# A gated cross-attention block: rows centred but not scaled before the scores, the deviation moved into the exponential's scale, and batch 1's low parts made by VectorE

## The chip, the cores and the metric

One NeuronCore of a Trainium2 chip runs the whole kernel. The metric is the device time of one execution in microseconds (us). Three runs of the kernel before gave 129.15, 129.49 and 129.62 us, median 129.49.

## The reference

Two batches of 1024 rows of 256 numbers go through one gated cross-attention layer and one gated feed-forward layer with fixed-point rounding. Only the first half is touched by the change.

```
h   = (x - mean(x)) / sqrt(var(x) + 1e-5)             # per row of 256
q   = h @ Wq;  k = ctx @ Wk;  v = ctx @ Wv             # 8 heads of 64, ctx has 77 rows
a   = softmax(q @ k.T / 8)                             # per head
x   = x + tanh(g_xattn) * (concat(a @ v) @ Wo + bo)
y   = (x - mean(x)) / sqrt(var(x) + 1e-5)
h1  = relu(quant(quant(y) @ quant(w1).T + quant(b1)))  # 1024 wide
x   = x + tanh(g_ffn) * (quant(h1) @ quant(w2).T + quant(b2))
```

## The kernel before, in words

The 2048 rows are 16 tiles T of 128 rows, eight per batch. Two products of weights with the short context are made once per batch: `a_sb` (Wq times the keys, 256 x 616, so that scores are one product of the row with it) and `u_sb` (the values times Wo, 640 x 256, so that the attention's output is one product of the probabilities with it). Both are kept as a high part in float32r and a low part, the rest that float32r leaves out; the rows and the probabilities are split in the same way, and each product is three products: high x high, high x low, low x high (`PARTS`). A high part is a copy out of PSUM by ScalarE (`a_copy`, `u_copy`, `xT_copy`, `pT_copy`). A low part is a subtraction by VectorE out of PSUM (`a_low`, `u_low`, `rowsT_low`, `probsT_low`).

Batch 1 departs from this at three places. For `a_sb` c = 0 and c = 1 and for the middle piece of `u_sb`, ScalarE makes a second, unrounded copy of the PSUM bank in SBUF (`full`, lines 488, 493, 499), and GpSimd subtracts the high part from it (`a_low`, `u_low` at lines 293 to 301). GpSimd cannot read PSUM. The semaphores `copied` and `copied_low` carry that.

Everything is written by hand, with one instruction stream for each engine and semaphores between them. A loop over s = 0 .. 15 is unrolled on all engines. In step s, TensorE makes: the transposes of the rows of tile s+3 (`rowsT`, line 728), the transposes of the probabilities of tile s (`probsT`, line 755), extra work in early steps (line 699 for batch 1's `a_sb` in steps 0 and 1, line 835, line 712 for batch 1's `u_sb` in step 3), from step 4 a half of the feed-forward's hidden layer (line 803), the transpose of the second norm's result of tile s-2 (`quantisedT`, line 784), from step 6 the second layer of the feed-forward (line 818), the scores of tile s+2 (line 743), and the attention's output of tile s (`attend`, line 776).

VectorE's step s: `residual(s-1)` (584), `stats_second(s-1)` (589, 591), `denominators(s+1)` (554, 557), `probsT_low(s)` (579), `rowsT_low(s+3)` (570), in steps 3 and 4 `u_low` of batch 1, from step 6 `result(s-6)` (596), in steps 1 to 5 the first norm's statistics of two tiles (534, 537), and `center(s+2)`, the maxima and their subtraction (542, 547).

GpSimd's step s: `normalise_first(s+4)` (272), `normalise_second(s-1)` (283, 284, 286, 290), `softmax_scale(s+1)` (277), a low part of batch 1 in steps 0, 1 and 3 (295, 300), the widening of the hidden layer's int8 (322), `add_bias(s-1)` (343). `rstd_first` (263, 264, 266), the first norm's deviation, comes in steps 2, 4 and 6, for 2, 4 and 4 tiles.

ScalarE's step s: `exponentials(s+1)` (396), `pT_copy(s)` (408), `xT_copy(s+3)` (392), copies and roundings of weights in some steps, `hidden_round` (422) and `rowsT_second` (428).

Ahead of the loop TensorE runs six matmuls of constants that nobody reads (`WARM`, line 685), then the context's transposes (854), the keys (692), Wq's transposes (868), batch 0's `a_sb` (699), the values in two halves (692), the transposes of tiles 0 and 1 (881), `scores(0)`, `rowsT(2)`, batch 0's `u_sb` (712) and `scores(1)`.

## Time and profile before

| | us |
|---|---|
| median of three runs | 129.49 |
| the profiled execution | 129.84 |
| its span on the engines | 127.9 |
| TensorE busy | 121.3 (95%) |
| VectorE busy | 99.8 (78%) |
| GpSimd busy | 93.7 (73%) |
| ScalarE busy | 71.3 (56%) |

The profiled execution took 129.84 us, of which 127.9 are the span from the first to the last instruction. Busy shares are averages over a start (up to 22 us), a loop and a tail, each with its own limit. TensorE's matmuls are pipelined, so that its 95% hides short waits; they are read from the start of one group of matmuls to the start of the next.

### The profile page before, as it was taken

What the parts mean: (1) busy time and instruction counts of PE and PEld (TensorE: products, weight loads), DVE (VectorE), ACT (ScalarE), POOL (GpSimd) and SP (SyncE); (2) the same over time, 40 slices, a digit from 0 to 9 for tenths busy, and PEclk for the clock granted to TensorE, in tenths of its full rate; (3) what the DMA queues carried; (4) which work ended last, traced back from release to release, by engine and by line L of the source; (5) the groups of instructions that cost most, each with busy time, mean ns of one, the idle gap of its engine ahead of it and who ended that gap; (6) DMA issues with size and microseconds to landing.
All of it is one profiled execution on the core that took longest, in us unless ns stands there. A gap on an engine that the chain in (4) does not pass through costs nothing.

```text
span 127.9 us, 2834 instructions
## 1 busy us (share of the span) xinstructions
PE 121.3 (95%) x996; PEld 110.4 (86%) x996; DVE 99.8 (78%) x221; ACT 71.3 (56%) x151; POOL 93.7 (73%) x175
## 2 busy tenths in 40 slices
PE   7999999999995999999999999999999999999990
PEld 2698978989893799999999899999999999888780
DVE  6109888599999879999897969697887979547882
ACT  4124625599793828499392829282837546365520
POOL 3002873777979898989998998988768596987720
PEclk9999999999999999999999999999999999999999
DMA  3898898100000000000002000200020020001014
GB/s 113 244 297 300 292 399 350 68 3 5 3 3 0 0 0 8 0 0 0 5 0 82 0 0 5 82 0 3 5 82 0 0 85 5 0 29 58 24 58 164
DMA packets 5572, 8.86 MB, mean 69 GB/s; under 512 B 1180, under 2 KB 2743, under 8 KB 5431
## 3 DMA queue, kind: packets, MB, share of 16 engines
q1 hardware_dynamic: 5559, 8.69, 19.2%
q8 instruction: 8, 0.13, 0.4%
q14 instruction: 5, 0.04, 0.1%
HBM read 6.59 MB, written 2.10 MB: 68 GB/s over the span
## 4 chain that ended last, share of the span: by engine, by line
PE 55%; POOL 27%; issue 7%; DVE 5%; DMA 2%; ACT 2%; POOLq 0%; DVEq 0%
PE of_ps L776 12%; PE sc_ps L743 11%; PE h_ps L803 7%; PE of_ps L818 6%; PE tr_ps L692 5%; PE tr_ps L755 4%; POOL rstd L286 4%; POOL yq L290 4%; POOL x_sb L343 3%; POOL probs L277 3%; POOL hid L322 3%; POOL xn L272 3%; DMA ctx_sb<-in_ctx_dram 2%; POOL rstd L266 2%; PE h_ps L712 1%
## 5 line engine op out<-in xcount | busy, mean ns | idle before, releaser
L776 PE MATMUL of_ps<-u_sb,pT 128*128 128x256 f32 x240 | 31.5, 282 | 0.3
L743 PE MATMUL sc_ps<-a_sb,xT 128*128 128x308 f32 x192 | 31.2, 311 | 0.0
L776 PEld LDWEIGHTS of_ps<-u_sb,pT 128*128 128x128 f32 x240 | 29.9, 188 | 1.0 <-issue 0.7
L743 PEld LDWEIGHTS sc_ps<-a_sb,xT 128*128 128x128 f32 x192 | 27.5, 189 | 0.8 <-issue 0.6
L422 ACT ACTIVATE hid_q<-h_ps,b1z 128x256 int8<-128x256 f32 x58 | 24.9, 495 | 3.9 <-PE h_ps L803 3.9
L396 ACT ACTIVATE probs<-probs 128x616 f32<-128x616 f32 x16 | 11.6, 722 | 27.7 <-DVE probs L547 27.7
L277 POOL TENSOR_TENSOR probs<-probs,rden 128x616 f32<-128x616 f32 x16 | 19.6, 1224 | 3.7 <-DVE rden L557 3.7
L542 DVE TENSOR_REDUCE mx<-sc_ps 128x8 f32<-128x616 f32 x16 | 12.7, 792 | 7.4 <-PE sc_ps L743 7.4
L322 POOL CAST hid<-hid_q 128x512 bf16<-128x512 int8 x27 | 15.9, 613 | 2.0 <-ACT hid_q L422 2.0
L803 PE MATMUL h_ps<-x2T,w1T 128*128 128x256 bf16 x128 | 16.6, 273 | 0.0
L408 ACT CAST pT<-tr_ps 128x640 fp32r<-128x640 f32 x16 | 11.0, 690 | 7.1 <-PE tr_ps L755 6.8
L803 PEld LDWEIGHTS h_ps<-x2T,w1T 128*128 128x128 bf16 x128 | 12.4, 98 | 1.6 <-ACT x2T L428 0.3
L579 DVE TENSOR_TENSOR pT<-tr_ps,pT 128x640 fp32r<-128x640 f32 x16 | 12.6, 790 | 0.8 <-ACT xT L392 0.5
L554 DVE TENSOR_REDUCE den<-probs 128x8 f32<-128x616 f32 x16 | 12.3, 766 | 1.3 <-ACT probs L396 1.3
L547 DVE TENSOR_TENSOR probs<-sc_ps,mx 128x616 f32<-128x616 f32 x16 | 12.8, 801 | 0.5
L755 PE MATMUL tr_ps<-ident,probs 128*128 128x128 f32 x80 | 11.5, 275 | 1.6 <-POOL probs L277 1.6
L818 PE MATMUL of_ps<-w2T,hid 128*128 128x256 bf16 x96 | 12.4, 273 | 0.0
L343 POOL TENSOR_TENSOR x_sb<-x_sb,b_gated 128x256 f32<-128x256 f32 x16 | 11.9, 741 | 0.0
L755 PEld LDWEIGHTS tr_ps<-ident,probs 128*128 128x128 f32 x80 | 9.1, 141 | 2.1 <-POOL probs L277 2.1
L584 DVE SCALAR_TENSOR_TENSOR x_sb<-of_ps,tg,x_sb 128x256 f32<-128x256 f32 x16 | 7.7, 481 | 4.1 <-PE of_ps L776 2.8
L290 POOL TENSOR_SCALAR yq<-x_sb,nm,rstd 128x256 int8<-128x256 f32 x16 | 9.0, 561 | 1.7
L286 POOL TENSOR_TENSOR rstd<-ve,mhalf 128x1 f32<-128x1 f32 x16 | 8.9, 554 | 1.3
(105 smaller groups left out, 184.7 us busy)
## 6 DMA issues: line engine op xcount, KB each, us to landing
w_sb<-in_L_ffn_w_dram SPq DMA_DIRECT2D x2, 1024.0 KB, 11.3
out_dram<-x_sb SPq DMA_DIRECT2D x7, 256.0 KB, 2.5
x_sb<-in_x_dram SPq DMA_DIRECT2D x4, 256.0 KB, 8.2
x_sb<-in_x_dram SPq DMA_DIRECT2D x1, 1024.0 KB, 11.5
wk_sb<-in_L_xattn_Wk_dram SPq DMA_DIRECT2D x2, 256.0 KB, 3.7
wq_sb<-in_L_xattn_Wq_dram SPq DMA_DIRECT2D x1, 512.0 KB, 5.9
wv_sb<-in_L_xattn_Wv_dram SPq DMA_DIRECT2D x1, 512.0 KB, 7.7
wo_sb<-in_L_xattn_Wo_dram SPq DMA_DIRECT2D x1, 512.0 KB, 7.7
```

The lines of the kernel that those rows point to most:

```text
L277: nc.gpsimd.tensor_tensor(probs_v(T), probs_v(T), rden[:, T % 2, :].unsqueeze(2).to_broadcast([P, H, M]), ALU.mult).then_inc(probs_ready, 1)
L286: nc.gpsimd.tensor_tensor(rstd2[:, i, :], ve2[:, i, :], mhalf[:, 0:1], ALU.pow).then_inc(rstd2_ready, 1)
L290: nc.gpsimd.tensor_scalar(yq[:, i, :], x_sb[:, T, :], nm2[:, i, 0:1], rstd2[:, i, 0:1], ALU.add, ALU.mult).then_inc(yq_ready, 1)
L322: nc.gpsimd.tensor_copy(hid[:, p, c:c + 2, :, :].rearrange("p c i r -> p (c i r)"), hid_q[:, (2 * k + n) % 4, :]).then_inc(hid_ready, 1)
L343: nc.gpsimd.tensor_tensor(x_sb[:, T, :], x_sb[:, T, :], b2_gated[:, :], ALU.add).then_inc(bias_added, 1)
L422: ins = nc.scalar.activation(hid_q[:, (2 * k + n) % 4, D * c:D * c + D], h_ps[:, n, D * c:D * c + D], ACT.Relu, bias=b1z[:, chunk:chunk + 1])
L547: nc.vector.tensor_tensor(probs_v(T).rearrange("p (a h) m -> p a h m", a=2), sc_v, mx[:, i, :].rearrange("p (a h) -> p a h", a=2).unsqueeze(3)
L743: ins = nc.tensor.matmul(sc_ps[:, a, 0:HALF], xT[:, T % 2, p, c, :], a_sb[:, q, T // TB, c, HALF * a:HALF * a + HALF], start=first, stop=last)
L755: ins = nc.tensor.transpose(pT_ps[:, P * c:P * c + P], probs[:, T % 2, P * c:P * c + P], ident[:, :])
L776: ins = nc.tensor.matmul(attn_ps, pT[:, T % 2, p, P * c:P * c + P], u_sb[:, q, MC * (T // TB) + c, :], start=first, stop=last)
L803: ins = nc.tensor.matmul(h_ps[:, n, D * c:D * c + D], w1T[:, d, P * chunk:P * chunk + P], x2T[:, p, d, :, :].rearrange("p i r -> p (i r)") ...
L818: ins = nc.tensor.matmul(ffn_of(T), hid[:, p, c, i, :], w2T[:, c, :], start=(c == 0), stop=(c == FC - 1))
```

## The change

1. The first norm loses its scaling. `normalise_first` and the negated mean on GpSimd are gone. For tiles 2 to 15 ScalarE writes mean - x (`minus_centred`); for tiles 0 and 1 VectorE does. Wq's transpose is copied with the factor -1/8 (`-SCALE`), and the exponential takes the row's `rstd1` as its scale, so that it waits for `rstd1_ready` too. GpSimd still makes `rstd1`, now two tiles at a time, in steps 3, 5, 7, 9 and 11.
2. Batch 1's three low parts that GpSimd made out of `full` are made by VectorE out of PSUM: `a_low(1, 0)` and `a_low(1, 1)` at the ends of steps 0 and 1, `u_low(1, 1)` in step 3. ScalarE's three copies into `full` are gone. TensorE waits for `a_ready` where it waited for `copied`.
3. VectorE's statistics of the first norm are spread, one tile in each of steps 1 to 10.
4. The start: the context comes in two DMAs, batch 0 from SP's queue and batch 1 from ScalarE's; `WARM` is 7; the transposes of tiles 0 and 1 come ahead of the values; the second half of the values comes behind `scores(0)`, its copies are ScalarE's instead of VectorE's, and `output_weights(0)` waits for them half-way; `scores(0)` waits for the low part of `a_sb` only ahead of its second part.

```diff
-WARM = 6
-FIRST_OF = (0, 2, 4, 6, 8, 12)
+WARM = 7
+FIRST_OF = tuple(range(0, TILES, 2))
...
-            sp.dma_start(ctx_sb[:, :, :], ctx_in.rearrange("b m d -> m b d")).then_inc(ctx_in_sb, 16)
+            sp.dma_start(ctx_sb[:, 0, :], ctx_in[0, :, :]).then_inc(ctx_in_sb, 16)
...
-                nc.gpsimd.tensor_scalar(nm1[:, t], mv1[:, t, 0], -1.0, 1.0, ALU.mult, ALU.mult).then_inc(ve1_ready, 1)
...
-            def normalise_first(T):
-                pool.wait_ge(rstd1_ready, T + 1)
-                if T >= 2:
-                    pool.wait_ge(xT_psum, T - 1)
-                nc.gpsimd.tensor_scalar(xn[:, T % 2, :], x_sb[:, T, :], nm1[:, T:T + 1], rstd1[:, T:T + 1],
-                                        ALU.add, ALU.mult).then_inc(xn_ready, 1)
...
-            def a_low(c, n):
-                pool.wait_ge(copied, n)
-                nc.gpsimd.tensor_tensor(a_sb[:, 1, 1, c, :], full[:, :], a_sb[:, 0, 1, c, :].bitcast(F32),
-                                        ALU.subtract).then_inc(copied_low, 1)
...
             for s in range(TILES):
-                if s == 2:
-                    rstd_first(6, 8)
-                if s == 4:
-                    rstd_first(8, 12)
-                if live(s + 4) and s > 0:
-                    normalise_first(s + 4)
                 if live(s - 1):
                     normalise_second(s - 1)
                 if live(s + 1):
                     softmax_scale(s + 1)
-                if s in (0, 1):
-                    a_low(s, s + 1)
-                if s == 3:
-                    u_low(1)
+                if s % 2 == 1 and 3 <= s < TILES - 4:
+                    rstd_first(s + 3, s + 5)
...
+            def minus_centred(T):
+                act.wait_ge(mv1_ready, T + 1)
+                act.wait_ge(xT_psum, T - 1)
+                nc.scalar.activation(xn[:, T % 2, :], x_sb[:, T, :], ACT.Identity, bias=mv1[:, T, 0:1],
+                                     scale=-1.0).then_inc(xn_ready, 1)
+
             def exponentials(T):
+                act.wait_ge(rstd1_ready, T + 1)
                 act.wait_ge(centered, T + 1)
-                nc.scalar.activation(probs_v(T), probs_v(T), ACT.Exp, scale=SCALE).then_inc(exp_done, 1)
+                nc.scalar.activation(probs_v(T), probs_v(T), ACT.Exp, scale=rstd1[:, T:T + 1]).then_inc(exp_done, 1)
...
+            act.dma_start(ctx_sb[:, 1, :], ctx_in[1, :, :]).then_inc(ctx_in_sb, 16)
             act.wait_ge(ctxT_psum, 1)
...
+            minus_centred(2)
+            minus_centred(3)
+            act.wait_ge(v_psum, 2)
+            for q in range(2):
+                nc.scalar.copy(head_blocks(vz, 1, q), pair_bank(0, q)).then_inc(v23_ready, 1)
             xT_copy(2)
+            exponentials(0)
             u_copy(0, 0)
-            exponentials(0)
             u_copy(0, 1)
             u_copy(0, 2)
+            minus_centred(4)
...
+                if live(s + 4) and s > 0:
+                    minus_centred(s + 4)
                 if s == 0:
                     a_copy(1, 0)
-                    nc.scalar.copy(full[:, :].rearrange("p (a m) -> p a m", a=2), a_banks[1, 0]).then_inc(copied, 1)
                     round_weights(w1_in, w1_sb, w1q, w1_rounded)
...
             stats_first(0, 2)
-            stats_first(2, 4)
+            for T in range(2):
+                dve.wait_ge(mv1_ready, T + 1)
+                nc.vector.tensor_scalar(xn[:, T, :], x_sb[:, T, :], mv1[:, T, 0:1], -1.0, ALU.subtract,
+                                        ALU.mult).then_inc(xn_first, 1)
...
-                if s in (3, 4):
-                    u_low(1, 2 * (s - 3))
+                if s == 3:
+                    u_low(1, 0)
+                    u_low(1, 1)
+                if s == 4:
+                    u_low(1, 2)
                 if live(s - 6):
                     result(s - 6)
-                if 1 <= s <= 5:
-                    stats_first(4 + 2 * s, 6 + 2 * s)
+                if 1 <= s and live(s + 5):
+                    stats_first(s + 5, s + 6)
                 if live(s + 2):
                     center(s + 2)
+                if s < DK:
+                    a_low(1, s)
...
-            pe.wait_ge(wv_in, 16)
-            keysT(wv_sb, v_psum, (0, 1))
             for T in range(2):
-                pe.wait_ge(xn_ready, T + 1)
+                pe.wait_ge(xn_first, T + 1)
...
-            keysT(wv_sb, v_psum, (2, 3))
-            pe.wait_ge(a_ready, 2)
+            pe.wait_ge(wv_in, 16)
+            keysT(wv_sb, v_psum, (0, 1), 0)
+            pe.wait_ge(a_high, 2)
+            pe.wait_ge(a_ready, 1)
             scores(0)
-            pe.wait_ge(v23_ready, 2)
+            pe.wait_ge(v01_ready, 2)
+            keysT(wv_sb, v_psum, (2, 3), 0)
             rowsT(2)
...
                 if s == 1:
                     weights1T()
-                    pe.wait_ge(copied, 1)
+                    pe.wait_ge(a_ready, DK + 1)
                     score_weights(1, 1)
                 if s == 3:
-                    pe.wait_ge(copied, 2)
+                    pe.wait_ge(a_ready, 2 * DK)
```

## Rows read from the trace of the kernel before

**Rows 1.** The page: the span, and the chain that ended last.

```profile
span 127.9 us, 2834 instructions
PE 55%; POOL 27%; issue 7%; DVE 5%; DMA 2%; ACT 2%; POOLq 0%; DVEq 0%
```

**Rows 2.** Timeline of the first 11 us: start, duration, engine, line, operation.

```profile
0.72 1.28 ACT L452 ACT_TABLE_LOAD   x1 [0.72 <-PEq L949]
0.76 2.72 PE L685 MATMUL of_ps<-const-bfloat16-1.0 128*128 128x512 bf16 x6 [0.76 <-PEq L949]
2.16 0.47 SPq L222 DMA_DIRECT2D wq_sb<-in_L_xattn_Wq_dram  x1
5.05 4.44 PE L692 MATMUL tr_ps<-ctxT,wk_sb 128*128 128x154 f32 x16
9.28 1.47 PE L868 MATMUL h_ps<-ident,wq_sb 128*128 128x128 f32 x8
```

**Rows 3.** The same stretch: the chain's DMA, and issue-to-landing times (wk's two, wq).

```profile
0.73 2.84 DMA ctx_sb<-in_ctx_dram
...
DMA to landing us min/median/max: 2.9/3.7/4.5
...
wq_sb<-in_L_xattn_Wq_dram SPq DMA_DIRECT2D x1, 512.0 KB, 5.9
```

**Rows 4.** Timeline of TensorE in the loop, same columns, chosen groups.

```profile
29.02 1.27 PE L699 MATMUL h_ps<-kz,wqT 128*128 128x154 f32 x8
34.98 1.94 PE L743 MATMUL sc_ps<-a_sb,xT 128*128 128x308 f32 x12
38.55 0.38 PE L728 MATMUL tr_ps<-ident,xn 128*128 128x128 f32 x2
40.36 0.77 PE L755 MATMUL tr_ps<-ident,probs 128*128 128x128 f32 x5 [1.43 <-POOL probs L277]
46.95 0.38 PE L728 MATMUL tr_ps<-ident,xn 128*128 128x128 f32 x2
69.97 0.38 PE L728 MATMUL tr_ps<-ident,xn 128*128 128x128 f32 x2
76.38 0.38 PE L728 MATMUL tr_ps<-ident,xn 128*128 128x128 f32 x2
82.44 0.38 PE L728 MATMUL tr_ps<-ident,xn 128*128 128x128 f32 x2
```

**Rows 5.** Timeline of VectorE in steps 1 and 2 of the loop.

```profile
28.82 0.47 DVE L584 SCALAR_TENSOR_TENSOR x_sb<-of_ps,tg,x_sb 128x256 f32<-128x256 f32 x1
29.33 0.43 DVE L589 BATCH_NORM_STATS2 st<-x_sb 128x6 f32<-128x256 f32 x1
...
29.89 0.76 DVE L554 TENSOR_REDUCE den<-probs 128x8 f32<-128x616 f32 x1
...
31.84 0.74 DVE L534 BATCH_NORM_STATS2 st<-x_sb 128x6 f32<-128x256 f32 x2
...
32.71 0.77 DVE L542 TENSOR_REDUCE mx<-sc_ps 128x8 f32<-128x616 f32 x1
...
34.23 0.47 DVE L584 SCALAR_TENSOR_TENSOR x_sb<-of_ps,tg,x_sb 128x256 f32<-128x256 f32 x1
```

**Rows 6.** Groups by line and form: busy, mean ns of one, idle before.

```profile
L561 DVE TENSOR_TENSOR a_sb<-sc_ps,a_sb 128x616 fp32r<-128x616 f32 x1 | 0.8, 799 | 0.3 <-ACT a_sb L400 0.3
L392 ACT CAST xT<-tr_ps 128x256 fp32r<-128x256 f32 x14 | 5.3, 376 | 1.6 <-PE tr_ps L728 1.6
L396 ACT ACTIVATE probs<-probs 128x616 f32<-128x616 f32 x16 | 11.6, 722 | 27.7 <-DVE probs L547 27.7
```

**Rows 7.** Timeline of GpSimd from step 1's end into step 2.

```profile
32.99 1.50 POOL L295 TENSOR_TENSOR a_sb<-full,a_sb 128x616 fp32r<-128x616 f32 x1
...
37.34 0.19 POOL L283 TENSOR_SCALAR ve<-mv 128x1 f32<-128x1 f32 x1
...
39.08 1.22 POOL L277 TENSOR_TENSOR probs<-probs,rden 128x616 f32<-128x616 f32 x1
```

More of the change, by code:

```diff
@@ L87, in flamingo_kernel @@
         u_sb = sb("u_sb", [P, 2, B * MC, D], F32R)
-        full = sb("full", [P, HM])
         w1q = sb("w1q", [P, FC, D], I8)
@@ L263, in rstd_first @@
                 nc.gpsimd.tensor_scalar(ve1[:, t], mv1[:, t, 1], EPS, 1.0, ALU.add, ALU.mult).then_inc(ve1_ready, 1)
-                nc.gpsimd.tensor_scalar(nm1[:, t], mv1[:, t, 0], -1.0, 1.0, ALU.mult, ALU.mult).then_inc(ve1_ready, 1)
-                pool.wait_ge(ve1_ready, 2 * len([T for T in FIRST_OF if T <= first]))
+                pool.wait_ge(ve1_ready, len([T for T in FIRST_OF if T <= first]))
                 nc.gpsimd.tensor_tensor(rstd1[:, t], ve1[:, t], mhalf[:, 0:end - first], ALU.pow).then_inc(rstd1_ready, end - first)
-            def normalise_first(T):
-                pool.wait_ge(rstd1_ready, T + 1)
-                if T >= 2:
-                    pool.wait_ge(xT_psum, T - 1)
-                nc.gpsimd.tensor_scalar(xn[:, T % 2, :], x_sb[:, T, :], nm1[:, T:T + 1], rstd1[:, T:T + 1],
-                                        ALU.add, ALU.mult).then_inc(xn_ready, 1)
             def softmax_scale(T):
@@ L291, in normalise_second @@
                                         ALU.add, ALU.mult).then_inc(yq_ready, 1)
-            def a_low(c, n):
-                pool.wait_ge(copied, n)
-                nc.gpsimd.tensor_tensor(a_sb[:, 1, 1, c, :], full[:, :], a_sb[:, 0, 1, c, :].bitcast(F32),
-                                        ALU.subtract).then_inc(copied_low, 1)
-            def u_low(n):
-                pool.wait_ge(copied, 3)
-                nc.gpsimd.tensor_tensor(u_of(1, n, 1), full[:, 0:2 * D], u_of(1, n, 0).bitcast(F32),
-                                        ALU.subtract).then_inc(copied_low, 1)
             def bias_rows():
@@ L379, in _ @@
                     add_bias(s - 1)
-                if s == 6:
-                    rstd_first(12, 16)
             normalise_second(TILES - 1)
@@ L458, in _ @@
                 act.wait_ge(wqT_psum, j + 1)
-                nc.scalar.copy(wqT[:, 2 * j:2 * j + 2, :].rearrange("p c n -> p (c n)"), h_ps[:, j, :]).then_inc(wqT_ready, 1)
+                nc.scalar.activation(wqT[:, 2 * j:2 * j + 2, :].rearrange("p c n -> p (c n)"), h_ps[:, j, :], ACT.Copy,
+                                     scale=-SCALE).then_inc(wqT_ready, 1)
             a_copy(0, 0)
@@ L491, in _ @@
                     a_copy(1, 1)
-                    act.wait_ge(copied_low, 1)
-                    nc.scalar.copy(full[:, :].rearrange("p (a m) -> p a m", a=2), a_banks[1, 1]).then_inc(copied, 1)
                     w1T_copy()
@@ L497, in _ @@
                     u_copy(1, 1)
-                    act.wait_ge(copied_low, 2)
-                    nc.scalar.copy(full[:, 0:2 * D], u_banks[1, 1]).then_inc(copied, 1)
                     u_copy(1, 2)
@@ L635, in _ @@
                                     ALU.subtract).then_inc(xT_ready, 2)
-            dve.wait_ge(v_psum, 2)
-            dve.wait_ge(vz_zero, 1)
-            for q in range(2):
-                nc.vector.tensor_copy(head_blocks(vz, 1, q), pair_bank(1, q)).then_inc(v23_ready, 1)
+            stats_first(2, 4)
             center(0)
+            stats_first(4, 6)
             rowsT_low(2)
+            denominators(0)
             u_low(0, 0)
-            denominators(0)
             u_low(0, 1)
@@ L686, in warm_up, with keysT @@
                                  nc.const_aps.tensor(1.0, [P, cols], BF16), start=True, stop=True)
-            def keysT(w, done, pairs):
+            def keysT(w, done, pairs, bank):
                 for j in pairs:
-                    at = 512 * (j // 2) + MP * (j % 2)
+                    at = 512 * bank + MP * (j % 2)
                     for c in range(DK):
@@ L710, in output_weights @@
                     c, row = g // (P // WIN), WIN * (g % (P // WIN))
+                    if (b, j, col) == (0, 2, 0):
+                        pe.wait_ge(v23_ready, 2)
                     dst = u_banks[b, c // 2][:, D * (c % 2):D * (c % 2) + D]
@@ L735, in scores @@
                 if T == TB:
-                    pe.wait_ge(copied_low, DK)
+                    pe.wait_ge(a_ready, 2 * DK)
                 for p, q in PARTS:
+                    if q == 1 and T == 0:
+                        pe.wait_ge(a_ready, 2)
                     if p == 1:
@@ L861, in _ @@
             pe.wait_ge(ctxT_ready, 1)
[L862 removed]
+            keysT(wk_sb, k_psum, (0, 1), 0)
             pe.wait_ge(wk_in[1], 16)
[L864 removed]
+            keysT(wk_sb, k_psum, (2, 3), 1)
             pe.wait_ge(wq_in, 16)
```

26 lines of the change are left out of this document (7 added, 19 removed).

## The prediction

> **What bounds the kernel now.** I read the chain of waits first: TensorE has 55% of it and GpSimd 27% [rows 1]. That looks like a kernel in which GpSimd's work is worth a quarter of the time. The next view corrects it. In TensorE's timeline I compared the start of each group with the start of the next, and looked for steps that are longer than the work in them. In the steady part a step takes 82.44 - 76.38 = 6.06 us with no hole. The step before it takes 76.38 - 69.97 = 6.41, so it holds a wait of 0.35. The large hole is in step 3: the rows' transposes start at 38.55, the probabilities' only at 40.36, though two transposes need 0.21; TensorE waits 1.6 us there for GpSimd's scale [rows 4]. So GpSimd runs late for 40 us, but makes TensorE wait for only about 2 us in sum. A chain that passes through an engine says that the engine was never early, not what its absence would bring. What can be won in the loop is the holes of TensorE, no more.
>
> VectorE is the third view. From 28.82 to 34.23 it works a step of 5.41 us without a stop [rows 5]: in steps 1 and 2 it is the engine that sets the pace, since TensorE has no feed-forward work yet. The change puts work onto just this engine in just these steps.
>
> **Part 1, the loop's early steps.** VectorE's step of 5.41 holds the statistics of two tiles, 32.71 - 31.84 = 0.87. One tile costs what the second norm's pair of instructions costs, 29.89 - 29.33 = 0.56 [rows 5]. So each of steps 1 and 2 is 0.31 shorter, 5.10. A low part out of PSUM took 0.80 in the start [rows 6]; neighbours overlap by some 0.05, so I take 0.75 (bounds 0.7, and 1.5, what GpSimd needs for it out of SBUF [rows 7]; the near row is the same instruction on the same engine, so I take that).
>
> - `a_low(1, 0)` stands behind the centring of tile 2, so `residual(0)` starts at 28.82 + 0.75 = 29.57. TensorE's line 699 of batch 1, c = 1, which started at 29.02 [rows 4], waits for it to 29.65.
> - Step 1 takes 5.10 + 0.75 = 5.85: `residual(1)` at 35.42 instead of 34.23, 1.19 late. TensorE needs it: `quantisedT(0)` and behind it the scores of tile 4, which start 34.98 - 34.23 = 0.75 behind its start. They go from 34.98 to 36.17, and step 2 ends at 38.55 + 1.19 = 39.74. So far the change loses 1.19 us.
> - Step 3: `probsT(3)` can start at 39.74 + 0.21 = 39.95 by TensorE. By GpSimd: its chain for tile 1 began at 37.34, though the statistics were done some 1.15 behind the residual, at 35.38 (the denominators, which follow them, start 29.89 - 28.82 = 1.07 behind [rows 5]); a low part of 1.50 from 32.99 on, an `add_bias`, deviations and a normalised row were in its queue [rows 7]. Of these only the `add_bias` is left there. Now it starts when VectorE delivers, 35.42 + 1.15 + 0.08 = 36.65; the scale follows 39.08 - 37.34 = 1.74 behind and takes 1.22, so it is done at 39.61. That is ahead of 39.95. `probsT(3)` starts at 39.95 instead of 40.36: 0.41 gained net, and with the 0.1 by which a restarted TensorE group was longer (0.77 against the usual 0.71), 0.5.
>
> The wait of 1.6 us on GpSimd is thus not simply won. Two thirds of it are paid out again as waits on VectorE one and two steps earlier.
>
> - Steps 3 to 5: VectorE gets `u_low(1, 1)` (0.80 x 512/616 = 0.65) and loses 0.31 a step. From 40.52 for `residual(2)`: 46.3 for `residual(3)` plus the 0.6 of `u_low(1, 0)` that was there before, 46.9. TensorE's step 3 ends at 46.95 - 0.5 = 46.45. So both are level, and VectorE is not late for the scores of step 4. After step 3 its step is shorter by 0.31 than it was, up to step 5.
> - Steps 6 to 10: VectorE now has statistics where it had none, 5.05 + 0.56 = 5.6 with `result` (5.05 = 5.41 - 0.87 + 0.5 for `result`). TensorE's 6.06 hides it; without that cover it would cost 0.56 a step.
> - Step 7's hole of 0.35 was GpSimd late after a `rstd_first` of four tiles. GpSimd's step was 5.4 plus that; without the row it is 4.8, or 5.9 with a `rstd_first` of two tiles, under 6.06 in both. Gained: 0.35.
>
> Loop: 0.5 + 0.35 = 0.85 gained (between 0.2, if VectorE's additions cost 0.3 more each, and 1.3).
>
> **Part 2, ScalarE.** It gets 14 rows, at between 0.38 (a copy of 256 columns out of PSUM) and 0.72 (an exponential of 616 columns in SBUF); the copy has the same width, so I take 0.4. It loses three copies into `full`. It sat idle 27.7 us ahead of its exponentials [rows 6], so 14 x 0.4 = 5.6 us of work fit. What stands behind `minus_centred` in its queue is `hidden_round`; TensorE wants that only in the next step. The exponential's new wait for `rstd1` is covered: GpSimd makes it two steps ahead. What a scale per row instead of a constant costs an exponential, no row shows; nothing in the steady steps waits for it, and in the early ones it could cost 0.1 each. I put all this at nothing, at most 0.3.
>
> In a sentence that the sum doesn't need: the Trainium skill ("ScalarE: Activation LUTs", Table sets: the hidden batching unit) says that cheap functions such as identity are in every table set; the trace has one load of 1.28 us for copy, relu, exp and tanh, and if Identity forced a reload each time, 14 pairs would cost 36 us, but no row shows that either way.
>
> **Part 3, the start.** From its first keys on TensorE has no hole of note, and the change alters the order, not the amount, of its work. The order only has to be free of new holes: `scores(0)` now starts right behind the copy of the transposed rows (a hole between nothing and one copy, 0.38 [rows 6]; I take 0.13), and the copies of the second values end before `output_weights(0)` is half-way. VectorE's centring of tiles 0 and 1 replaces GpSimd's and is earlier. The seventh constant matmul ends at about 0.76 + 7 x 0.43 = 3.8, where the context's data were there at 0.73 + 2.84 = 3.57 [rows 2, 3]: 0.07 more. Cost: 0.2.
>
> TensorE's clock is the open item. The sixteen key matmuls start 0.264 us apart ((9.28 - 5.05)/16), while line 699 with the same 154 columns runs in 1.0 us for eight, 0.125 each [rows 2, 4] (34.98 and 29.02 are both past the rise). So TensorE ran at the lower of its two levels, 1.2 GHz, from its first matmul to about 10.0, in the midst of line 868, and at 2.4 GHz afterwards. Before that it had one hole, from the end of the sixth constant matmul at 3.48 to the context, and nearly none from there. The seventh matmul fills this hole. Whether the rise then comes earlier, no row shows. Lower bound of the effect: nothing. Upper bound: a rise at 6.6 instead of 10.0 would save half of 3.4, 1.7 us; Wq landed at 2.16 + 5.9 = 8.1 [rows 2, 3], so the keys' end at 7.9 would still be in step with the loads.
>
> The DMA split: what the trace shows is that the context landed 2.84 after its issue, wk's halves 2.9 and 4.5 after theirs [rows 3]. So half a context on another queue lands between 0.73 + 2.8 = 3.5 and 0.73 + 4.5 = 5.2. I take 3.6, since it is the smallest and first transfer; then the constants hide it. The Trainium skill ("DMA: Bandwidth & Descriptors", Issuing engines are not separate DMA queues) speaks against the split: transfers issued by several engines share the same 16 DMA engines and only the time to issue is saved. By that rule it brings nothing, which is the value taken; the trace, with one queue only, can't test it.
>
> **Sum.** 0.85 - 0.2 = 0.65 us less. The profiled execution took 129.84, so it would be 129.2; on the median, 129.49 - 0.65 = 128.8.
>
> **The rivals.**
>
> - *The clock rises early.* TensorE is busy without a break from 0.76, and the rise comes at some 6.6. For it: the one hole is filled. Against it: the hole was only 0.2 of the 9 us that TensorE needed up to the rise, and the gap before the keys is still there. 0.65 + 1.7 = 2.35 less: 127.1.
> - *The half context lands late and the clock with it* (the other side). ScalarE's queue mixes its half with the weights, and it lands like wk's second half at 5.2, or the table load of 1.28 [rows 2] goes ahead of it. The keys then start at 6.5 instead of 5.05. If the rise shifts by as much as the keys' start, it comes at 11.5: 16 keys and most of line 868 at half speed end at 12.0 instead of 10.5, 1.5 lost, 0.85 more than gained: 130.3. It decides from a landing at about 4.5. If the rise stays at 10.0, the loss is only 0.7 and the time is that of before.
> - *VectorE takes it all.* The added work in steps 0 to 3 costs 0.3 more for each low part, or the exponentials come late, and TensorE leaves step 3 where it did before, at 46.95. Then only step 7's 0.35 is left, less the start's 0.2: 129.4, no change. For it: VectorE had no idle time in steps 1 and 2. Against it: the durations are those of the same instructions.
>
> **How the numbers follow.** The forecast with its own range 128.4 to 129.2: 0.42. The early clock: 0.28. VectorE takes it: 0.17. The late context: 0.13. About 0.5% (0.65 us) is what a measurement of this kernel can tell from no change, and the forecast lies just on it, so half of it counts as faster: 0.23 + 0.28 gives 0.51 faster; 0.19 + 0.17, and a little of the late context, 0.38 the same; 0.11 slower. The range reaches from the early clock, 126.9, to between no change and the late context, 129.9.
>
> **What would show it.** In the changed kernel's profile: the wait on GpSimd in step 3 gone, and waits of about 0.6 (line of batch 1's `a_sb`) and 1.0 (`quantisedT(0)`) on VectorE in its place; step 3 ending 0.5 earlier; steps from 4 on at TensorE's own pace, 6.06 from step 6; VectorE's step at 5.6 in steps 6 to 10; the keys' spacing of 0.264 up to about 10.0 (an early change to 0.13 means the first rival); the context's landing under 3.8. I am wrong if TensorE still waits for GpSimd, if ScalarE's rows delay the hidden layer, or if the start differs by over 0.5.

## The result and the profile after

The changed kernel took 128.03 us (median, 127.93 to 128.10) beside 129.40 (129.15 to 129.62) for the kernel before: a ratio of 0.989, 95% interval 0.986 to 0.992, so 1.1% faster. Forecast were 128.8 and a gain of 0.65. The sign was right and the range of 126.9 to 129.9 holds the time. But the gain is 1.37, twice the forecast, and it doesn't come from where I expected it: two errors of opposite sign lie inside it, so that the range holds the time in part by luck.

The page of the changed kernel, with busy time, share and instructions of each engine, and the chain that ended last:

```profile
span 126.1 us, 2846 instructions
PE 119.6 (95%) x997; PEld 108.8 (86%) x997; DVE 101.9 (81%) x224; ACT 77.1 (61%) x164; POOL 80.6 (64%) x154
PE 75%; DVE 10%; DMA 5%; ACT 3%; issue 3%; POOL 1%; SPq 1%; DVEq 0%; POOLq 0%; ACTq 0%
```

GpSimd's share of the chain fell from 27% [rows 1] to 1%, its busy time by 13 us, and the profiled execution became 1.8 us shorter in span (127.9 to 126.1; 127.98 us beside 129.84). As the prediction said, that share was not what could be won.

The timeline of TensorE in the changed kernel (start, duration, engine, line, operation; lines 667, 674, 681, 712, 729, 741, 761, 769, 852 are what 685, 692, 699, 728, 743, 755, 776, 784, 868 were before):

```profile
0.76 3.15 PE L667 MATMUL of_ps<-const-bfloat16-1.0 128*128 128x512 bf16 x7 [0.76 <-PEq L933]
3.70 0.72 PE L838 MATMUL sc_ps<-ident,ctx_sb 77*128 77x77 f32 x4
5.02 2.38 PE L674 MATMUL tr_ps<-ctxT,wk_sb 128*128 128x154 f32 x16
8.05 1.10 PE L852 MATMUL h_ps<-ident,wq_sb 128*128 128x128 f32 x8 [0.66 <-DMA wq_sb<-in_L_xattn_Wq_dram]
...
20.35 0.38 PE L712 MATMUL tr_ps<-ident,xn 128*128 128x128 f32 x2
...
28.24 1.32 PE L681 MATMUL h_ps<-kz,wqT 128*128 128x154 f32 x8 [0.51 <-DVE a_sb L538]
...
34.51 0.22 PE L769 MATMUL of_ps<-ident_b,yq 128*128 128x128 bf16 x1 [0.69 <-DVE x_sb L561]
...
38.20 0.38 PE L712 MATMUL tr_ps<-ident,xn 128*128 128x128 f32 x2
38.42 0.71 PE L741 MATMUL tr_ps<-ident,probs 128*128 128x128 f32 x5
...
44.99 0.38 PE L712 MATMUL tr_ps<-ident,xn 128*128 128x128 f32 x2
...
50.51 0.38 PE L712 MATMUL tr_ps<-ident,xn 128*128 128x128 f32 x2
...
74.39 0.38 PE L712 MATMUL tr_ps<-ident,xn 128*128 128x128 f32 x2
...
80.47 0.38 PE L712 MATMUL tr_ps<-ident,xn 128*128 128x128 f32 x2
```

What to see: the hole ahead of the probabilities of step 3 [rows 4] is gone, 38.42 follows 38.20 at once. In its place stand the two waits on VectorE, 0.51 and 0.69. And the loop begins at 20.35, where it began at 21.86 before.

Here and below a step is measured from the start of its rows' transposes (728, now 712) to the next; "the start" is everything ahead of step 0; "the loop" is from there to the attend of tile 15. All are read from TensorE's timeline, in us:

| | start | step 0 | 1 | 2 | 3 | 4 | 5 | 8 | 9 to 11 | loop |
|---|---|---|---|---|---|---|---|---|---|---|
| before | 21.86 | 5.93 | 5.83 | 4.93 | 8.40 | 5.25 | 5.67 | 6.41 | 6.05 | 91.63 |
| after | 20.35 | 6.01 | 6.54 | 5.30 | 6.79 | 5.52 | 5.71 | 6.06 | 6.06 | 91.28 |

Of the 1.86 by which the last matmuls came earlier, 1.51 lie in the start and 0.35 in the loop. Forecast were -0.2 and +0.85. So there were two questions: why the start gained, and where the loop's other 0.5 went.

The traces of all the runs below give the scatter of these two numbers. The kernel before, with its tiles where they are, has loops of 91.63, 91.49, 91.48 and 91.66 in four executions, the changed kernel 91.28, 91.28, 91.22 and 91.29 (and 91.52 in a fifth, under a lowered clock). So the loop gained between 0.2 and 0.4. What is left of a time when the start and the loop are taken off is nearly fixed: 16.2 to 16.45 in the ten traces outside the frame that is explained below. By that, an estimate, the median of 129.24 (34 executions of the kernel before, taken beside the first runs below) and the 128.03 stand for starts of some 21.4 and 20.4: a gain of 1.0 in the start of the typical execution, not 1.5.

### The profile page after: what moved, and what is told of

Its sections match the earlier page's. It is cut to its first block, busy times and chain, and to the rows that moved or that the text cites. A ratio compares the mean times of both kernels' runs of the same rounds, so it can differ in the third digit from the quotient of the medians.

```text
span 126.1 us, 2846 instructions
## 1 busy us (share of the span) xinstructions
PE 119.6 (95%) x997; PEld 108.8 (86%) x997; DVE 101.9 (81%) x224; ACT 77.1 (61%) x164; POOL 80.6 (64%) x154
## 4 chain that ended last, share of the span: by engine, by line
PE 75%; DVE 10%; DMA 5%; ACT 3%; issue 3%; POOL 1%; SPq 1%; DVEq 0%; POOLq 0%; ACTq 0%
PE sc_ps L729 19%; PE of_ps L761 19%; PE h_ps L787 9%; PE of_ps L802 7%; PE tr_ps L741 6%; DMA wq_sb<-in_L_xattn_Wq_dram 5%; PE h_ps L696 3%; PE tr_ps L712 2%; DVE probs L524 2%; DVE mx L519 2%; PE tr_ps L674 2%; PE tr_ps L802 1%; DVE den L531 1%; ACT probs L368 1%; DVE a_sb L538 1%
## 5 line engine op out<-in xcount | busy, mean ns | idle before, releaser
L368 ACT ACTIVATE probs<-probs,rstd 128x616 f32<-128x616 f32 x16 | 13.0, 814 | 26.1 <-DVE probs L524 26.1
L272 POOL TENSOR_SCALAR ve<-mv 128x1 f32<-128x1 f32 x16 | 3.1, 192 | 15.7 <-DVE mv L568 15.6
L260 POOL TENSOR_SCALAR ve<-mv 128x2 f32<-128x2 f32 x8 | 1.6, 196 | 14.1 <-DVE mv L514 13.7
```

What stands on the lines that cost most here:

```text
L368: nc.scalar.activation(probs_v(T), probs_v(T), ACT.Exp, scale=rstd1[:, T:T + 1]).then_inc(exp_done, 1)
```

## Experiments: the start

The two candidates that the prediction had named were the seventh constant with an earlier clock, and the context's DMA in halves. First each alone, put into the kernel before and taken out of the changed one.

The kernel before with seven constants:

```
-WARM = 6
+WARM = 7
```

> The kernel before with a seventh constant matmul and nothing else. Theory A (the seventh matmul closes TensorE's hole ahead of the context, and that brings the clock's rise forward): keys 0.13 us apart instead of 0.264 from the start or soon after it, about 1.5 us less than before. Rival B (the earlier rise needs the context to be there when the constants end, which the split DMA brings): as before within 0.2 us, keys at 0.264 up to about 10. Rival C (the rise is by chance from one execution to the next): the times of this kernel spread over more than 1 us.

Measured: 129.08 (128.64 to 129.99), ratio 0.999 [0.996, 1.002]: nothing.

The changed kernel with six:

```
-WARM = 7
+WARM = 6
```

> The changed kernel with six constant matmuls. Theory A: the keys are at 0.264 again and the kernel loses 1.5 us against the changed one, so 0.2 faster than the kernel before at the most. Rival B: no change against the changed kernel (128.0), since the context has landed when the sixth ends.

Measured: 128.07 (127.5 to 128.9), ratio to before 0.993 [0.990, 0.996], beside 128.03 with seven: nothing that can be told from zero.

The kernel before with the context in two halves, the second from ScalarE's queue:

```
-            sp.dma_start(ctx_sb[:, :, :], ctx_in.rearrange("b m d -> m b d")).then_inc(ctx_in_sb, 16)
+            sp.dma_start(ctx_sb[:, 0, :], ctx_in[0, :, :]).then_inc(ctx_in_sb, 16)
...
+            act.dma_start(ctx_sb[:, 1, :], ctx_in[1, :, :]).then_inc(ctx_in_sb, 16)
...
-            pe.wait_ge(ctx_in_sb, 16)
+            pe.wait_ge(ctx_in_sb, 32)
```

> The kernel before with the context in two DMAs, six constant matmuls. Theory A: TensorE has a hole still if the context lands after 3.5, then the time is that of before. Rival B: the context lands by 3.4, TensorE goes from the constants straight into the transposes, keys 0.13 us apart, about 1.5 us less than before.

Measured: 129.33 (128.16 to 129.48), ratio 1.001 [0.998, 1.004]: nothing.

The changed kernel with the context in one DMA (the reverse of the edit above):

> The changed kernel with the context in one DMA, seven constant matmuls. Theory A: as the changed kernel, 128.0, clock high from the keys on. Rival B: the kernel loses about 1.5 us.

Measured: 128.31 (128.02 to 130.56), ratio to before 0.994 [0.991, 0.996]. The changed kernel with six constants, on the same chip, has 128.07 and 0.993; the 0.24 between them lies inside the spread of either.

Neither candidate moves the median: in each of the four runs the alternative with no change held, and the one with 1.5 us did not. But the traces of this set show what moves. TensorE's timeline in the kernel before with the halved context:

```profile
3.63 0.74 PE L855 MATMUL sc_ps<-ident,ctx_sb 77*128 77x77 f32 x4 [0.15 <-DMA ctx_sb<-in_ctx_dram]
4.97 2.34 PE L693 MATMUL tr_ps<-ctxT,wk_sb 128*128 128x154 f32 x16
7.15 1.03 PE L869 MATMUL h_ps<-ident,wq_sb 128*128 128x128 f32 x8
```

The same sixteen key matmuls that took 4.44 us in the profiled execution of before [rows 2] take 2.34 here, with six constants and the hole still there; with seven constants in before they took 2.97, in the changed kernel 2.38. So the step from the lower rate to the higher falls at changing times from one execution to the next. In four traces of before's order it came at the keys' start, twice within the keys, and once (the profile of before) only in the middle of Wq's transposes. In the changed kernel it came within the keys at the latest (2.83 for them with padding), and at the earliest ahead of the context's transposes, which took 0.43 instead of 0.72. The granted clock of the profile doesn't show this step: it reads 1.00 in every microsecond from 1 to 16 of before. The lower level is read here from the spacing of the matmuls alone, 0.264 beside 0.125 for the same 154 columns.

The profile of before had caught the latest rise of them all. It is tempting to put the whole scatter of the single executions (128.17 to 130.01 for the kernel before) down to this. The table further down shows a second source, which in these four traces is the larger.

To take both the clock and the loads out of the comparison, the next set put a frame around each kernel: 22 constants, and TensorE waits for the rows' first load ahead of the context's transposes, so that nearly all loads are there when the work begins.

```
-WARM = 6
+WARM = 22
...
             pe.wait_ge(ident_set, 1)
+            pe.wait_ge(x_in[0], 16)
             pe.wait_ge(ctx_in_sb, 16)
```

The kernel before in this frame:

> The kernel before with 22 constant matmuls and a wait for tiles 0 and 1 ahead of the context's transposes, so that the real work starts at about 9.5 with the clock already at its high level. Theory C (the clock's rise falls by chance somewhere between 4 and 10 us, and that is what spreads the times of one kernel over 1.5 us): the times spread over less than 0.6 us; keys 0.13 us apart. About 2 us slower than before. If the spread stays, its cause is another.

Measured: 132.53 (132.23 to 134.95; five of the six within 0.37). The keys took 2.34. The loop begins 12.41 behind the start of Wq's transposes and takes 91.66.

The changed kernel in this frame (the same edit, WARM 7 to 22):

> The changed kernel in the same frame (22 constants, the same wait). The difference to b_fix is what the change is worth at equal clocks. Theory: 0.4 to 0.9 us faster than b_fix, 0.5 of it in the loop, spread under 0.6. Rival (the change is worth the 1.4 us of the first comparison without the clock): 1.4 faster.

Measured: 133.88 (131.82 to 135.53). As a comparison of medians this failed (forecast was 0.4 to 0.9 faster than b_fix). TensorE's timeline and a row of the windows (stretch, busy, granted clock, DMA share, GB/s):

```profile
10.89 0.46 PE L839 MATMUL sc_ps<-ident,ctx_sb 77*128 77x77 f32 x4 [3.22 <-issue]
11.95 3.84 PE L674 MATMUL tr_ps<-ctxT,wk_sb 128*128 128x154 f32 x16 [0.27 <-ACT ctxT L425]
...
11.00:13.00 2.00, 1.73 (x10) 0.65 0.80 264
```

Here TensorE idled for 3.2 us ahead of the context's transposes (the page names no releaser; the wait for the rows is what the edit put there), and after it the granted clock fell: 0.65 on average between 11 and 13 us, 0.50 from 12 to 15, the keys back at 3.84. The loop's length can still be read, 91.29, the same as without the frame, and it begins 12.27 behind Wq's transposes. So with the loads there, the two orders of the start differ by only 0.14 (12.41 against 12.27). That is close to what the prediction had assumed, and it is not what happens without the frame.

An explanation came with two executions whose Wq transposes begin within 0.1 us of each other, 8.04 and 7.95, both past the rise: the kernel before with one tile declared elsewhere (the edit stands in the last section of experiments) and the changed kernel once more. VectorE and TensorE of the first (in brackets the idle time before the row, and what ended it):

```profile
9.16 0.75 DVE L534 BATCH_NORM_STATS2 st<-x_sb 128x6 f32<-128x256 f32 x2 [0.69 <-DMA x_sb<-in_x_dram]
12.24 0.75 DVE L534 BATCH_NORM_STATS2 st<-x_sb 128x6 f32<-128x256 f32 x2 [2.10 <-DMA x_sb<-in_x_dram]
13.24 0.80 DVE L561 TENSOR_TENSOR a_sb<-sc_ps,a_sb 128x616 fp32r<-128x616 f32 x1
...
14.80 2.29 PE L743 MATMUL sc_ps<-a_sb,xT 128*128 128x308 f32 x12 [0.38 <-DVE a_sb L561]
```

And of the changed kernel:

```profile
9.17 0.75 DVE L511 BATCH_NORM_STATS2 st<-x_sb 128x6 f32<-128x256 f32 x2 [1.11 <-DMA x_sb<-in_x_dram]
10.05 0.60 DVE L606 TENSOR_SCALAR xn<-x_sb,mv 128x256 f32<-128x256 f32 x2
11.36 0.80 DVE L538 TENSOR_TENSOR a_sb<-sc_ps,a_sb 128x616 fp32r<-128x616 f32 x1 [0.70 <-ACT a_sb L372]
...
13.00 1.94 PE L729 MATMUL sc_ps<-a_sb,xT 128*128 128x308 f32 x12
```

In the order of before, VectorE stands for 2.1 us at the statistics of tiles 2 and 3, whose rows have not landed; the low part of `a_sb`, whose high part was there at 11.40, is queued behind them and starts at 13.24, and TensorE's first scores wait for it. In the changed order these statistics come behind both low parts. Eight executions put a number on it:

| | tiles 2, 3 landed (statistics start) | Wq's transposes | loop begins | behind Wq's | behind the statistics |
|---|---|---|---|---|---|
| before | 11.77 | 9.28 | 21.86 | 12.58 | 10.09 |
| before, halved context | 11.08 | 7.15 | 20.48 | 13.33 | 9.40 |
| before, seven constants | 12.24 | 7.82 | 21.64 | 13.82 | 9.40 |
| before, tile declared late | 12.24 | 8.04 | 21.64 | 13.60 | 9.40 |
| after | | 8.05 | 20.35 | 12.30 | |
| after, again | | 7.95 | 20.24 | 12.29 | |
| after, six constants | | 8.46 | 20.73 | 12.27 | |
| after, with padding | | 7.68 | 19.93 | 12.25 | |

The changed start is always 12.3 behind Wq's transposes here. That of before is the later of some 12.5 behind Wq's transposes and 9.40 behind the landing of tiles 2 and 3. It also answers the question of the scatter: between the kernel with the halved context (128.16) and the two below it, the start differs by 1.16, and so does the landing of tiles 2 and 3; the late rise in the profile of before put its start 0.22 behind theirs, and 0.69 behind what its own landing allowed (11.77 + 9.40 = 21.17). (The changed kernel with one DMA is left out of the table: behind a hole of 1.60 us its two groups of batch 0's `a_sb` took 2.23 and 2.01 us instead of 1.32 and 1.21, the lower level again, and the granted clock reads 0.50 from 11 to 13 us.) This is read from traces, not from an experiment that moved the statistics alone; none of the runs did only that. Nor does a run show which of the two limits the typical execution of before met: its estimated start of 21.4 fits a landing at 12.0, and equally Wq's transposes at 8.9.

## Experiments: the loop

Six further runs, two in the frame and four outside it, take the change's parts apart. First, in the frame, both places where the new work stood in the way moved: `a_low(1, 0)` ahead of `center(2)`, `a_low(1, 1)` into step 2, and `minus_centred` behind `hidden_round`:

```
-                if live(s + 4) and s > 0:
-                    minus_centred(s + 4)
...
                     hidden_round(s - 4, 1)
+                if live(s + 4) and s > 0:
+                    minus_centred(s + 4)
...
+                if s == 0:
+                    a_low(1, 0)
+                if s == 2:
+                    a_low(1, 1)
                 if live(s + 2):
                     center(s + 2)
-                if s < DK:
-                    a_low(1, s)
```

> a_fix with two orders altered: a_low(1, 0) ahead of the centring of tile 2, a_low(1, 1) in step 2 ahead of the centring of tile 4, and minus_centred behind hidden_round and rowsT_second on ScalarE. Theory (what the loop lost are waits for VectorE of 0.5 in step 1 and 0.7 in step 2, and of 0.24 in step 4 for ScalarE's copy): 0.4 to 1.2 us faster than a_fix. Rival (VectorE's amount of work sets the pace, not its order): within 0.2 of a_fix.

Measured: 131.89 (131.57 to 134.70); the medians can't be compared, since that of a_fix failed; the loop is 90.86, 0.43 shorter. Step 2 went from 5.32 to 4.70, so the wait on VectorE there was real. New waits took part of it back:

```profile
37.05 0.44 PE L714 MATMUL tr_ps<-ident,xn 128*128 128x128 f32 x2 [0.49 <-ACT xn L362]
...
52.49 2.04 PE L763 MATMUL of_ps<-u_sb,pT 128*128 128x256 f32 x15 [0.28 <-ACT x2T L400]
```

The centred rows, now behind the weights' copies in ScalarE's queue, are late for TensorE once; and step 4's wait for `x2T` is still there though `minus_centred` has gone from in front of it; the step grew from 5.52 to 5.78. That doesn't clear `minus_centred`: VectorE was later too, so that the exponential of step 4 started 1.10 behind the step's beginning (49.69 - 48.59) instead of 0.44. It shows that `minus_centred` isn't needed for the wait.

Second, part 2 of the change undone in the frame: the three low parts back on GpSimd, with ScalarE's copies into `full`, all else as changed.

```
+        full = sb("full", [P, HM])
...
+            def a_low(c, n):
+                pool.wait_ge(copied, n)
+                nc.gpsimd.tensor_tensor(a_sb[:, 1, 1, c, :], full[:, :], a_sb[:, 0, 1, c, :].bitcast(F32),
+                                        ALU.subtract).then_inc(copied_low, 1)
...
+                if s in (0, 1):
+                    a_low(s, s + 1)
+                if s == 3:
+                    u_low(1)
...
-                    u_low(1, 1)
...
-                if s < DK:
-                    a_low(1, s)
```

> a_fix with part 2 undone: batch 1's three low parts on GpSimd again, with ScalarE's copies into full. Theory (their move to VectorE cost 1.2 us in steps 1 and 2, and without the normalised rows GpSimd has room for them): 0.3 to 0.8 us faster than a_fix. Rival (GpSimd's low parts are what made TensorE wait 1.6 us in step 3): 0.5 or more slower than a_fix, with that wait back.

Measured: 130.74, of a wide spread (129.57 to 133.16) as in the changed kernel in the frame; the loop 89.23, 2.06 shorter than 91.29, where 0.3 to 0.8 was forecast. The steady steps took 6.00 in it instead of 6.06, which no part of the arithmetic explains. `full` had come back, and with it the addresses of every tile declared behind it. The last set takes the two apart, without the frame.

Part 2 undone (the same edit, on the changed kernel):

> The changed kernel, its own start, with part 2 undone (batch 1's three low parts on GpSimd). From the framed pair: its loop was 2.05 us shorter than the changed kernel's (89.23 against 91.28), 1.2 of it in steps 1 and 2, 0.25 in step 4, the rest 0.06 in each later step. Theory (VectorE's low parts cost 1.2 to 1.5, and the 0.06 a step is where the tiles lie in SBUF, since full is declared again): 126.0, with attend at 1.72 us. Rival (the 0.06 a step belongs to that chip): 126.6, attend at 1.78.

Measured: 126.12 us (125.52 to 126.88), ratio to before 0.975 [0.972, 0.978]; loop 89.31.

The changed kernel with a tile that nothing uses, at `full`'s place:

```
         u_sb = sb("u_sb", [P, 2, B * MC, D], F32R)
 
+        full = sb("full", [P, HM])
```

> The changed kernel with the tile full declared again and used by nobody, which moves every tile declared behind it by 2464 bytes a partition and changes no instruction. Theory (TensorE's attend depends on where pT lies in SBUF): attend 1.72 us instead of 1.78, the loop 0.6 to 1.0 shorter, 127.2. Rival (chip or chance): the same as the changed kernel.

Measured: 127.15 (126.96 to 127.60), ratio 0.983 [0.981, 0.986]; loop 90.71, so 0.57 shorter, just under the forecast 0.6.

The kernel before with `nm1` (64 bytes in a partition) declared last:

```
-        nm1 = sb("nm1", [P, TILES])
...
         hid = sb("hid", [P, TP, FC, 2, P], BF16)
 
+        nm1 = sb("nm1", [P, TILES])
```

> The kernel before with the tile nm1 declared last, which moves xn, xT, probs, pT and what follows down by 64 bytes a partition, to the addresses that they have in a_pad. Theory of the addresses: attend 1.72 instead of 1.77, 0.5 to 1.0 faster than before. Rival: no difference.

Measured: 129.06 (128.51 to 129.49), ratio 0.998 [0.995, 1.001]; loop 91.32. The forecast of 0.5 to 1.0 was missed, and the median can't tell it from no change. The loop is 0.31 shorter than in the profile of before and 0.16 shorter than the shortest of its four. What stands clear of that scatter are the steady steps, 6.00 instead of 6.03 to 6.07, and the attend, 1.71 instead of 1.78. Part of the gain is lost again in step 8, where the wait for GpSimd's scale grew (6.61 instead of 6.32 to 6.43).

The changed kernel once more, as the reference of this set:

> The changed kernel once more, for more executions beside the three above. Theory (the clock's rise falls by chance, in the kernel before too): its times spread over 1 us or more, and its median is 0.5 to 1.2 under that of before. Rival (the changed start brings the early rise each time): all within 0.3 of 128.0.

Measured: 128.02 (127.12 to 128.54), ratio 0.989 [0.986, 0.992]; loop 91.28.

In the first three of these, `probs`, `pT` and their neighbours lie at the same addresses. TensorE's timeline of the attend (line 761 and its like) in the steady steps, first the changed kernel with padding, then the changed kernel:

```profile
78.01 1.88 PE L762 MATMUL of_ps<-u_sb,pT 128*128 128x256 f32 x15
79.73 0.38 PE L713 MATMUL tr_ps<-ident,xn 128*128 128x128 f32 x2
84.01 1.88 PE L762 MATMUL of_ps<-u_sb,pT 128*128 128x256 f32 x15
```

```profile
78.67 1.96 PE L761 MATMUL of_ps<-u_sb,pT 128*128 128x256 f32 x15
80.47 0.38 PE L712 MATMUL tr_ps<-ident,xn 128*128 128x128 f32 x2
84.72 1.96 PE L761 MATMUL of_ps<-u_sb,pT 128*128 128x256 f32 x15
```

The same fifteen matmuls on the same data are 1.72 us ahead of what follows them with the padding (79.73 - 78.01), 1.80 without it (80.47 - 78.67), and the step is 6.00 instead of 6.05. The kernel before does the same with the 64 bytes moved: 1.71 beside 1.78. By loop lengths: the padding is worth 91.28 - 90.71 = 0.57, and at equal addresses the lists read

| at the padded addresses | step 1 | 2 | 3 | 4 | 5 | 8 | loop |
|---|---|---|---|---|---|---|---|
| before | 5.80 | 4.89 | 8.37 | 5.21 | 5.62 | 6.61 | 91.32 |
| changed | 6.49 | 5.33 | 6.70 | 5.61 | 5.66 | 6.00 | 90.71 |
| changed, part 2 undone | 5.82 | 4.80 | 6.79 | 5.32 | 5.62 | 6.00 | 89.31 |

So part 2 by itself costs 1.40 us of the loop: 0.67, 0.53 and 0.29 in steps 1, 2 and 4. It gains 0.09 in step 3, whose wait on GpSimd is gone without it too (6.79 beside 8.37). The removal of GpSimd's normalised rows and the negated mean had freed it already. Its timeline with the low part back:

```profile
28.59 0.19 POOL L274 TENSOR_SCALAR ve<-mv 128x1 f32<-128x1 f32 x1 [0.94 <-DVE mv L589]
...
31.51 1.52 POOL L286 TENSOR_TENSOR a_sb<-full,a_sb 128x616 fp32r<-128x616 f32 x1
...
33.80 0.19 POOL L274 TENSOR_SCALAR ve<-mv 128x1 f32<-128x1 f32 x1
```

It carries the 1.52 us and still begins `ve` of the next tile 0.2 us behind VectorE's statistics (33.41 + 0.18), where in step 2 of before it began 2 us behind them [rows 7]. The medians went from 127.15 to 126.12, 1.03; in the profiled pair the start of the kernel with part 2 undone is 0.37 later (20.30 against 19.93), and 1.40 - 0.37 is 1.03 (the two profiled times differ by 0.90). The kernel with part 2 undone is the fastest of all here, 3.2 us under the one before.

## Why the prediction was right or wrong

Times of a step are taken from the beginning of the loop, so that the start drops out.

**The wait for `a_low(1, 0)`: right.** TensorE's batch 1 `a_sb` group stood 29.02 - 21.86 = 7.16 behind the loop's beginning and now stands 28.24 - 20.35 = 7.89 behind it, 0.73 later; forecast 0.63, and 0.08 of it is the longer step 0. (As idle time in brackets it is 0.51.)

**Step 1 of VectorE and the end of step 2: right.** VectorE of the changed kernel:

```profile
28.11 0.47 DVE L561 SCALAR_TENSOR_TENSOR x_sb<-of_ps,tg,x_sb 128x256 f32<-128x256 f32 x1
...
33.19 0.79 DVE L538 TENSOR_TENSOR a_sb<-h_ps,a_sb 128x616 fp32r<-128x616 f32 x1
33.90 0.47 DVE L561 SCALAR_TENSOR_TENSOR x_sb<-of_ps,tg,x_sb 128x256 f32<-128x256 f32 x1
```

`residual(1)` is 33.90 - 20.35 = 13.55 behind the loop's beginning, before it was 34.23 - 21.86 = 12.37: 1.18 later, forecast 1.19. VectorE's step is 5.79, forecast 5.85. Step 2 ends 1.16 late, forecast 1.19. These rows carried the argument, since they are the same instructions on the same engine, back to back.

**Step 3: right.** `probsT(3)` stands 18.07 behind the beginning, before 18.50: 0.43 gained, forecast 0.41. Its end gained 0.45, forecast 0.5. GpSimd's scale began at 36.87 and took 1.22, so that it was done 17.74 behind the beginning (forecast 39.61 - 21.86 = 17.75), 0.33 ahead of TensorE.

**Step 4: wrong, by 0.27.** The prediction called TensorE and VectorE level here, and ScalarE's part nothing, with up to 0.3. They were level, and that is the point: without slack every delay goes through. The term that was mis-sized is the delay of the attend in this step, put at nothing (ScalarE's part with at most 0.3). VectorE makes two low parts of `u_sb` in step 3, and the exponential of step 4 starts 0.44 behind the step's beginning instead of 0.10. ScalarE of the changed kernel in step 4:

```profile
45.43 0.81 ACT L368 ACTIVATE probs<-probs,rstd 128x616 f32<-128x616 f32 x1 [2.70 <-DVE probs L524]
46.15 0.67 ACT L380 CAST pT<-tr_ps 128x640 fp32r<-128x640 f32 x1
46.72 0.38 ACT L356 CAST xT<-tr_ps 128x256 fp32r<-128x256 f32 x1
46.98 0.52 ACT L362 ACTIVATE xn<-x_sb,mv 128x256 f32<-128x256 f32 x1
47.40 0.84 ACT L394 ACTIVATE hid_q<-h_ps,b1z 128x256 int8<-128x256 f32 x2
48.11 0.39 ACT L400 CAST x2T<-of_ps 128x256 bf16<-128x256 int8 x1
```

The copy of `x2T` empties `of_ps`, into which the attend writes. It ends at 48.50, and the attend starts at 48.64 instead of 48.45 (1.80 behind the scores, which start at 46.65): 0.19. The other 0.08 is that an attend which had to wait takes 1.87 up to the next group instead of 1.79. The failed sentence is "what stands behind `minus_centred` is `hidden_round`": `rowsT_second` stands there too. With part 2 undone, `minus_centred` and the dearer exponential are still there and step 4 takes 5.32 beside 5.21: so some 0.1 is ScalarE's. The other 0.3 at equal addresses goes with part 2; that it comes through VectorE's lateness is read from the rows.

**ScalarE's prices.** `minus_centred` took 518 ns (forecast 0.4, bounds 0.38 and 0.72), the exponential with a scale per row 814 ns instead of 722 [rows 6] (forecast "0.1 each"). From step 5 on nothing waits for them: right. There is one table load of 1.28 us in the changed kernel, as before, so Identity costs no load of a table; the rule of the Trainium skill ("ScalarE: Activation LUTs", Table sets: the hidden batching unit) holds here.

**Steps 6 to 10 and the hole of 0.35: right.** It is 6.06 now where it was 6.41. By the numbering of the tables it is step 8's, the prediction called it step 7's.

**The loop's sum: 0.35 instead of 0.85, in the profiled pair.** Step 4 is 0.27 of the missing 0.5; step 0, where the attend waits 0.19 for `pT`'s low part, 0.08; the rest is a few hundredths a step. Addresses enter this sum too: the changed kernel pays 0.57 for its own and the kernel before 0.16 to 0.34 (its four loops against 91.32), so the removed tiles cost some 0.2 to 0.4, and at equal addresses the loop gained 91.32 - 90.71 = 0.61, one execution of each, within the forecast's 0.2 to 1.3. No step of the prediction had a term for that.

**The start: wrong, and the largest error (1.51 gained in the profiled pair, 0.2 lost by forecast).** By the prediction's own words ("I am wrong ... if the start differs by over 0.5") this refutes its account of the start. The failed step is "the change alters the order, not the amount, of its work". The working asked whether the new order opens holes on TensorE, not whether the old order held one for VectorE. The profile of before didn't show it: there the late clock had put the keys' end at 9.28, so that tiles 2 and 3 kept VectorE waiting for only 0.18 us. In the profiled pair, then, the order gained nothing at all. TensorE before and after, in that order:

```profile
10.99 1.32 PE L699 MATMUL sc_ps<-kz,wqT 128*128 128x154 f32 x8 [0.24 <-ACT wqT L459]
```

```profile
9.40 1.32 PE L681 MATMUL sc_ps<-kz,wqT 128*128 128x154 f32 x8 [0.25 <-ACT wqT L432]
```

From batch 0's first `a_sb` group to the loop it is 21.86 - 10.99 = 10.87 before and 20.35 - 9.40 = 10.95 after. The whole 1.51 lies ahead of that group, in keys and Wq's transposes at the lower level in one execution and not in the other. In a pair with nearly the same clock and arrival of Wq (the tile declared late, and after, again), the starts differ by 21.64 - 20.24 = 1.40; up to the same group they differ by 9.37 - 9.30 = 0.07, and the other 1.33 is VectorE's queue. In the medians the start must account for about 1.37 - 0.35 = 1.0. So the 1.51 of one pair and the 1.0 of the medians are alike in size by chance. How the 1.0 is shared out between the queue and the rise stays open, since no run moved the statistics alone.

**The rival with the early clock** had 127.1. In the profiled pair its sign was there (keys 0.13 apart) and the start's 1.51 is its mechanism. As an effect of the change it isn't shown: seven constants or six make no difference that the medians of either kernel can tell, and three of four traces of before's order have an early rise too. Four traces are too few to say that a late rise is as frequent in both kernels. Where the rise is early, an earlier one brings nothing, since Wq's arrival bounds what follows (the 0.66 in the row of Wq's transposes); so the time was 128.0 and not 127.1. The 6.6 at which this rival put the rise stood in no row. **The late half of the context** fell: the transposes of the context start at 3.70 in the changed kernel, behind the constants. The rule of the Trainium skill ("DMA: Bandwidth & Descriptors", Issuing engines are not separate DMA queues), that a second issuing engine brings no bandwidth, agrees with 129.33 beside 129.24. **VectorE takes it all** was the nearest in its mechanism: the added work did cost 1.40 us at equal addresses. Its price was set against the wrong alternative, though. I credited part 2 of the change with GpSimd's relief, when the relief came from its part 1, the normalised rows.

## What to carry to other kernels

When a change has two parts that unload the same engine, price each with the other already done: here the second moved 0.8 us pieces onto the engine that set the pace in order to relieve one that had room by then, and it cost 1.4 us of 128. In an in-order queue look for an instruction that waits for a load with work behind it whose inputs are ready, and look at more than one execution, since a late clock or an early load hides it. And when a tile is added or removed, try the kernel with its bytes padded before the difference is put down to the change.

## What the runs showed of the hardware

- **Addresses in SBUF.** A tile of 2464 bytes in a partition that no instruction touches makes the same attend 1.72 us instead of 1.80, each steady step 6.00 instead of 6.06, and the loop 0.57 us shorter. A tile of 64 bytes moved to the end makes it 1.71 instead of 1.78, and 6.00 instead of 6.03 to 6.07, in the kernel before. The medians with the padding, 127.15 beside 128.02, differ by more; 0.3 of the profiled difference is the earlier beginning of Wq's transposes (7.68 against 7.95). By the 64-byte move the addresses of `a_sb`, `u_sb` and the feed-forward's weights are out, since they stayed. Which of the tiles behind them it is, and by what mechanism, stays open: `rstd1`, `xn`, `xT`, `probs`, `pT` and all behind them moved together.
- **TensorE's clock at the start.** The same sixteen matmuls took 4.44, 2.97, 2.83, 2.60, 2.38 or 2.34 us in executions of nearly the same program, according to when the step from the lower level (1.2 GHz) to the higher (2.4 GHz) fell; the granted clock in the profile reads 1.00 on both sides of it. The level came back down behind idle stretches of 3.22 us (in the frame) and 1.60 us (the changed kernel with one DMA), and there the granted clock does show it, at 0.50. One execution is not a basis for any number of this stretch.
- **Landings.** The rows of tiles 2 and 3 let VectorE begin at 11.08, 11.77 or 12.24, in kernels whose loads differ at most by the halved context. Where Wq's arrival ended TensorE's wait, its transposes began at 7.95 to 8.75; with no such wait at 7.15.
